# Distance products on half the array's rows each, with operands built by scaled copies

## The reference, cut to what matters

```python
s = x @ w_se.T + b_se                       # 3 numbers a node
sq = jnp.sum(s * s, axis=-1)
dist = sq[:, :, None] + sq[:, None, :] - 2.0 * jnp.einsum('bnd,bmd->bnm', s, s)
A = jnp.exp(-dist) * mask                   # mask: the adjacency, 512 x 512
msg = jax.nn.relu(x @ w_msg.T + b_msg)
x_nmp = jnp.einsum('bnm,bmd->bnd', A, msg)
```

## Time and profile before

| | |
|---|---|
| median of three runs | 655.06 us |
| the profiled execution | 653.34 us |
| its span, first to last instruction | 651.4 us |
| mean granted TensorE clock | 0.986 |
| TensorE matmuls busy | 606.5 us (93%), 3742 instructions |
| TensorE weight loads busy | 522.7 us (80%) |
| VectorE busy | 495.5 us (76%) |
| ScalarE busy | 410.2 us (63%) |
| GpSimd busy | 339.2 us (52%) |

### The profile page before, as it was taken

How to read it: one execution, slowest core, us unless ns; L and a number is a source line. 1 busy time by engine, 2 the same in 40 slices (tenths; PEclk the granted TensorE clock), 3 DMA queues, 4 the chain that set the end, 5 groups by cost and what they waited for, 6 DMA issues and landing times.

```text
span 651.4 us, 12656 instructions
## 1 busy us (share of the span) xinstructions
PE 606.5 (93%) x3742; PEld 522.7 (80%) x3742; DVE 495.5 (76%) x2023; ACT 410.2 (63%) x810; POOL 339.2 (52%) x250
## 2 busy tenths in 40 slices
PE   3899998989899999999999999999999999999990
PEld 2779777877779798989898988788888878999980
DVE  6968888798878888888888898888887856544430
ACT  4654545464849485858585858576676747777760
POOL 3200405042448446666757575748585853555675
PEclk9998999999999999999999999999999999999996
DMA  8427231317283997464665656555656677777553
GB/s 294 150 80 263 77 123 53 98 60 240 61 237 62 280 278 214 92 189 125 151 168 152 166 133 178 141 152 155 169 134 165 175 182 170 174 178 170 115 77 40
DMA packets 91715, 99.63 MB, mean 153 GB/s; under 512 B 7488, under 2 KB 70464, under 8 KB 91328
## 3 DMA queue, kind: packets, MB, share of 16 engines
q1 hardware_dynamic: 69920, 82.30, 40.3%
q0 software_dynamic: 21728, 16.53, 16.7%
HBM read 74.89 MB, written 30.39 MB: 162 GB/s over the span
## 4 chain that ended last, share of the span: by engine, by line
PE 81%; DVE 7%; ACT 5%; issue 4%; POOL 1%; DMA 1%; another core or an unknown queue 1%; POOLq 0%; SPq 0%; DVEq 0%; ACTq 0%
PE G L717 9%; PE Y L607 8%; PE C L541 8%; PE C L539 8%; PE C L540 7%; PE G L539 5%; PE G L541 5%; PE G L540 5%; PE G L607 3%; PE Y L615 3%; PE H L582 2%; PE H L584 2%; PE H L583 2%; PE M L545 2%; PE C L711 2%
## 5 line engine op out<-in xcount | busy, mean ns | idle before, releaser
L988 POOL DMA_INDIRECT out<-y_t,xt x88 | 144.3, 1639 | 117.7 <-DMA out<-y_t,xt 76.7
L1023 POOL DMA_INDIRECT routed<-row,at_u x112 | 126.7, 1131 | 137.1 <-DVE at_u L1220 104.8
L539 PE MATMUL C<-cv_h,w_hi 128*128 128x256 f32 (+1 forms) x432 | 131.7, 305 | 6.2 <-issue 3.7
L540 PE MATMUL C<-cv_l,w_hi 128*128 128x256 f32 (+1 forms) x432 | 125.2, 290 | 0.0
L541 PE MATMUL C<-cv_h,w_lo 128*128 128x256 f32 (+1 forms) x432 | 125.1, 290 | 0.0
L539 PEld LDWEIGHTS C<-cv_h,w_hi 128*128 128x128 f32 x432 | 83.6, 194 | 9.6 <-issue 6.4
L540 PEld LDWEIGHTS C<-cv_l,w_hi 128*128 128x128 f32 x432 | 83.5, 193 | 1.4
L541 PEld LDWEIGHTS C<-cv_h,w_lo 128*128 128x128 f32 x432 | 83.3, 193 | 0.7
L717 PE MATMUL G<-ex,msg_t 128*128 128x512 f32 x128 | 58.9, 603 | 0.3 <-ACT gh L911 0.3
L607 PE MATMUL Y<-ge,w_t 128*128 128x256 f32 x212 | 55.0, 382 | 3.1 <-issue 2.6
L607 PEld LDWEIGHTS Y<-ge,w_t 128*128 128x128 f32 x212 | 37.8, 189 | 12.8 <-issue 9.1
(11 more groups left out here) (265 smaller groups left out, 1679.6 us busy)
## 6 DMA issues: line engine op xcount, KB each, us to landing
w_t<-w_all SPq DMA_DIRECT2D x63, 392.0 KB
adj<-adj_t SPq DMA_DIRECT2D x16, 1024.0 KB
xt<-routed SPq DMA_DIRECT2D x63, 144.0 KB
wd<-w_all SPq DMA_DIRECT2D x11, 392.0 KB
x_ln<-x SPq DMA_DIRECT2D x16, 256.0 KB
x_res<-x SPq DMA_DIRECT2D x16, 256.0 KB
out<-x SPq DMA_DIRECT2D x15, 256.0 KB
w_all<-w_s SPq DMA_DIRECT2D x1, 3136.0 KB, 11.3
```

Of the source, the lines that this page charges most:

```text
L539: pe.matmul(psum, hi(w), rhs_h, start=start, stop=False)
L540: pe.matmul(psum, hi(w), rhs_l, start=False, stop=False)
L988: nc.gpsimd.indirect_dma_start(out=out, out_offset=bass.IndirectOffsetOnAxis(ap=xt[j][:, t, R_ID:R_ID + 1].bitcast(U32), axis=0), in_=y_t[ ...
L1023: nc.gpsimd.indirect_dma_start(out=routed, out_offset=bass.IndirectOffsetOnAxis(ap=ats_u[d % 2][:, n:n + 1], axis=0), in_=rows[d % 2][:, n ...
```

## The change

The eight groups of three rows stand in 32-row blocks 0 and 32 of the first half, and again in the second half. The first block holds s, the second s squared, in each half. ScalarE evicts G2 in four activations of 32 partitions in place of two of 64. The casts become two activations over all 128 partitions with a scale and a bias column from the constants, which also write the constant rows; the VectorE steps become two sums over all partitions. `dist(j)` uses rows 0 to 63 for even j and rows 64 to 127 for odd j, and the wait for `msg_done` stands before `dist(2)`. The two memsets and their semaphore are gone; ScalarE waits once for the constants.

```diff
-S_ROWS = [0, SPACE, 2 * SPACE, 3 * SPACE, 64, 64 + SPACE, 96, 96 + SPACE]
+S_HALF = [0, SPACE, 2 * SPACE, 3 * SPACE, 32, 32 + SPACE, 32 + 2 * SPACE, 32 + 3 * SPACE]
+S_ROWS = [half + row for half in (0, 64) for row in S_HALF]
...
             def dist(j):
-                pe.matmul(DIST[j][:], u_s[:, j * P:(j + 1) * P], v_s[:], start=True, stop=True).then_inc(pe_dist, 1)
+                rows = slice(64 * (j % 2), 64 * (j % 2) + 64)
+                pe.matmul(DIST[j][:], u_s[rows, j * P:(j + 1) * P], v_s[rows, :], start=True, stop=True).then_inc(
+                    pe_dist, 1)
...
-                if is_graph(g, 0):
-                    pe.wait_ge(rows_set, 1)
...
+                pe.wait_ge(msg_done, g + 1)
                 dist(2)
-                pe.wait_ge(msg_done, g + 1)
                 dist(3)
...
-                nc.scalar.activation(s_f[0:64, :], G2[0:64, :], ACT.Identity, bias=vec[0:64, V_SE:V_SE + 1])
-                nc.scalar.activation(s_f[64:P, :], G2[64:P, :], ACT.Square,
-                                     bias=vec[64:P, V_SE:V_SE + 1]).then_inc(s_f32, 1)
+                for half in (0, 64):
+                    places, squares = slice(half, half + 32), slice(half + 32, half + 64)
+                    nc.scalar.activation(s_f[places, :], G2[places, :], ACT.Identity, bias=vec[places, V_SE:V_SE + 1])
+                    last = nc.scalar.activation(s_f[squares, :], G2[squares, :], ACT.Square,
+                                                bias=vec[squares, V_SE:V_SE + 1])
+                last.then_inc(s_f32, 1)
                 tile_results(-1)
                 act.wait_ge(s_f32, g + 1)
-                nc.scalar.copy(u_s[0:96, :], s_f[0:96, :])
-                nc.scalar.copy(v_s[0:64, :], s_f[0:64, :])
-                nc.scalar.copy(v_s[96:P, :], s_f[96:P, :]).then_inc(uv_hi, 1)
+                nc.scalar.activation(u_s[:], s_f, ACT.Identity, scale=cst[:, C_SU:C_SU + 1], bias=cst[:, C_BU:C_BU + 1])
+                nc.scalar.activation(v_s[:], s_f, ACT.Identity, scale=cst[:, C_SV:C_SV + 1],
+                                     bias=cst[:, C_BV:C_BV + 1]).then_inc(uv_hi, 1)
...
             act.wait_ge(vec_loaded, 16)
+            act.wait_ge(cst_loaded, 16)
...
-            def stack(tile, src, pattern, a=0, b=P):
-                return nc.vector.scalar_tensor_tensor(out=tile[a:b, :], in0=tile[a:b, :].bitcast(F32),
-                                                      scalar=cst[a:b, pattern:pattern + 1], in1=src[a:b, :],
-                                                      op0=ALU.mult, op1=ALU.add)
+            def low_halves(tile, scale):
+                return nc.vector.scalar_tensor_tensor(out=tile[:], in0=s_f, scalar=cst[:, scale:scale + 1],
+                                                      in1=tile[:].bitcast(F32), op0=ALU.mult, op1=ALU.add)
...
-                stack(u_s, s_f, C_DU, 0, 96)
-                stack(v_s, s_f, C_DV, 0, 64)
-                stack(v_s, s_f, C_DV, 96, P).then_inc(uv_split, 1)
+                low_halves(u_s, C_AU)
+                low_halves(v_s, C_AV).then_inc(uv_split, 1)
...
-            nc.vector.memset(u_s[96:P, :].bitcast(F32), -0.5)
-            nc.vector.memset(v_s[64:96, :].bitcast(F32), -0.5).then_inc(rows_set, 1)
```

More of the change, by code:

```diff
@@ L85 @@
 C_TRI = C_ID + P
-C_DU = C_TRI + P
-C_DV = C_DU + 1
-C_IOTA = C_DV + 1
+C_SU, C_BU, C_AU, C_SV, C_BV, C_AV = range(C_TRI + P, C_TRI + P + 6)
+C_IOTA = C_AV + 1
 C_HALF = C_IOTA + EXPERTS + 1
@@ L129, in constants @@
     c[:, C_TRI:C_TRI + P] = np.triu(np.ones((P, P)), 1)
[L130 to L134, removed]
+    for row, u, v in zip(S_HALF, ("h", "h", "l", "l", "sh", "sl", "one", "one"),
+                         ("h", "l", "h", "l", "one", "one", "sh", "sl")):
+        for half in (0, 64):
+            at = slice(half + row, half + row + SPACE)
+            for columns, kind in (((C_SU, C_BU, C_AU), u), ((C_SV, C_BV, C_AV), v)):
+                c[at, columns] = {"h": (1.0, 0.0, 0.0), "l": (-1.0, 0.0, 1.0), "sh": (-0.5, 0.0, 0.0),
+                                  "sl": (0.5, 0.0, -0.5), "one": (0.0, 1.0, 0.0)}[kind]
     c[:, C_IOTA:C_IOTA + EXPERTS] = np.arange(EXPERTS)
@@ L305, in gnn_moe @@
         conv_summed = sem("conv_summed")
-        zeroed, rows_set = sem("zeroed"), sem("rows_set")
+        zeroed = sem("zeroed")
         dv_step, dv_pow = sem("dv_step"), sem("dv_pow")
```

## The result

The changed kernel is slower. Its median is 662.84 us (four runs, 659.29 to 666.94), that of the kernel before 655.20 (four runs, 652.9 to 655.95): a ratio of 1.012 with the interval 1.007 to 1.017, or +7.6 us. The forecast was 671.5 (660 to 679): +16.4 on the median of before, where +7.6 was measured. The profiled executions are 659.62 and 653.34 us, +6.3, with spans of 657.8 and 651.4 and a granted clock of 0.986 in both.

The account below looks back on a forecast made before the run. TensorE was taken as the bound, with no slack behind ScalarE's evictions in graphs 6 to 15. 13.7 + 4.3 - 0.7 - 1.8 + 1.7 = +17.2 us on 653.34 gave 670.5, set at 671.5 us (660 to 679).

Parts of the forecast that it names:

- The step that held: Graphs 6 to 15, ScalarE's G2 evictions ahead of L821 and L615: 1.37 us more each, nothing covered, +13.7 us.
- the rival that went faster: G2 evictions cost by partitions, so the stage keeps its length: 644 to 650 us, chance 0.06.
- Its turning point: Added G2 eviction stage at which the faster rival turns: about 0.4 us a graph.
- The products: Four distance products a graph: -0.11 us as middle of -0.46 and +0.24, -1.8 us in 16 graphs.
- The rival that pairing pays in full: Distance products gain all of 7.4 us: 659 to 664 us, still slower, chance 0.20.
- The rival of costly changes of mode: Distance products at +3.8 in place of -1.8, up to one more clock fall: 675 to 679 us, chance 0.12.
- The copies: ScalarE's two scaled copies for three casts: 0.75 us each, 1.50 against 1.79, a gain of 0.29.
- The step that failed: Graphs 2 to 5, TensorE's waits for messages or gelu: each grows by 1.08 us, +4.3 us.
- the clock: Early graphs, TensorE at 1.2 GHz after pauses: one further clock fall, +1.7 us (0 to 5).
- the step's low end: Early graphs' waits: 0 added if the remote event that ScalarE next waits for comes at its own time.
- the sum's base: Profiled execution of the kernel before, 653.34 us, to which the summed +17.2 us was added, giving 670.5.
- Graph 0: VectorE's two sums for three: TensorE's wait for the last falls away in graph 0 only, -0.7 us.

Follow-up runs that it names:

- four_evictions: Kernel before with only its two 64-partition evictions of G2 cut into four of 32 partitions: 664.76 us beside 646.58, ratio 1.028.
- results_mid: Changed kernel with the tile's yT eviction moved between the second and third of the four evictions of G2: 652.42 us beside 646.58, ratio 1.010.
- full_rows: Changed kernel with each distance product over all 128 rows, exponential scale 1: 660.34 us beside 644.40 for the kernel before, ratio 1.025.
- base_third: Kernel before, unchanged, third profile, on a third chip: 653.78 us beside 654.06, ratio 1.000.
- base_again: Kernel before, unchanged, run again for a second profile: 648.78 us beside 646.58, ratio 1.003.
- after_third: Changed kernel, unchanged, third profile, on the same chip as the kernel before's third profile: 663.56 us, ratio 1.014 to the kernel before.
- after_again: Changed kernel, unchanged, run again for a second profile: 662.40 us, ratio 1.025 to the kernel before, +15.8 us.
- four_evictions_b: Kernel before with four 32-partition evictions of G2 in place of two of 64, run again on another chip: 666.87 us, ratio 1.026.

## Why the prediction was right in sign and too large

**The step that held.** L821 and L615 had no slack in graphs 6 to 15, and each added microsecond of ScalarE's stage there became one of TensorE: +1.37 a stage, waits of 1.50, graphs +1.30. four_evictions shows it with that part alone (34.73 - 33.36 = 1.37), results_mid by taking the wait away. The rows were enough to forecast it. Narrower activations cost what wide ones do, 671 and 681 ns for 32 partitions, so the rival that went faster falls. (Its turning point was summed wrongly: by its own terms it lies at (1.8 + 1.2 + 0.7) / 14 = 0.26 us a graph, not at 0.4.)

**The products held.** -0.11 a graph was forecast, -0.08 measured (full_rows). Both bounds' reasons were at work: pairing (-0.45) and the change to half the rows (+0.37). That their sum lies so near the middle is luck, for the middle was taken only because no row told more. The rival that pairing pays in full falls, although its 659 to 664 us held the time: right by its number, for another reason. The rival of costly changes of mode falls too.

**The copies** took 0.80 in place of 0.75, so that stage shrank not by 0.29: from the first copy to the gelu in the changed kernel it is 197.82 - 196.41 = 1.41 against 1.79, -0.38. The second copy starts 0.71 after the first, although each row is 0.80 long. Starts, not durations, add up.

**The step that failed** is the one on the early graphs: +4.3, of which I wrote "I take the full value, for the gap follows directly on ScalarE's last instruction, as if begun by it", with +1.7 for the clock on top. The waits did grow, by 1.13 each. But the gap was not begun by ScalarE's last instruction. It ended with an event at its own time, as the step's low end had it ("if that event comes at its own time, it swallows the delay"). The event can be named. L890 waits for the semaphore, a counter between engines, that TensorE raises with the last product of `conv_sum` (L541); what it needs of VectorE had ended long before (134.87 for the L890 at 139.21). The packed trace holds the time of each raise. The table has it in us from the graph's first eviction of G2, beside the end of what ScalarE does before L890. L541 itself ends at 3.69 in graphs 2 to 4 and at 4.58 in graph 5, in every row (ends on TensorE are modelled).

| | ScalarE free, graphs 2 to 4 | semaphore, graphs 2, 3, 4 | ScalarE free, graph 5 | semaphore, graph 5 |
|---|---|---|---|---|
| before | 4.35 | 5.15, 5.88, 5.87 | 6.64 | 7.95 |
| base_third | 4.35 | 5.15, 5.11, 5.88 | 6.64 | 7.92 |
| base_again | 4.35 | 4.25, 4.29, 4.27 | 6.65 | 7.84 |
| after | 5.49 | 5.13, 5.10, 5.10 | 7.78 | 7.96 |
| after_third | 5.48 | 5.14, 5.12, 5.12 | 7.78 | 7.96 |
| after_again | 5.49 | 4.35, 4.30, 4.26 | 7.78 | 7.87 |
| four_evictions_b | 5.73 | 4.25, 4.27, 4.28 | 8.02 | 7.84 |

The semaphore comes 0.6 to 3.4 us behind the product, and how late goes by the comparison more than by the kernel: after and after_third have it as late as before and base_third mostly do, and do not pause, for their ScalarE gets there after it. In graphs 3 and 4 of before and 4 of base_third it came another 0.75 later, at 5.87 or 5.88; as an estimate, such a one would leave the changed kernel a pause of 5.88 - 5.49 = 0.4. In the four profiles of the second chip it comes 0.01 behind the product, and there graph 5 has no pause in any kernel.

In numbers, for graphs 2 to 5. Without pauses in graphs 2 to 4 and without falls of the clock (after_again against base_again) the change costs +1.8 where +4.3 less 0.4 for the products was forecast: the semaphore swallows graph 5's part, and waits that stood behind the delay another 0.8 in graph 4. The 3.8 us of pauses that before has are no longer there. The clock gave +1.2 where +1.7 was forecast: graphs 2 and 5 of after hold a stretch at the lower level (from 79.7 and 165.0) and take 28.69 and 35.98 where those of after_again take 27.18 and 34.77, together +2.7, against the 1.5 of graph 3 before (111.1). 1.8 - 3.8 + 1.2 = -0.8, as measured. (Outside these graphs, graph 1 has such a stretch only before, from 49.6, which gives 0.6 back; over the early graphs both profiles have two.) Against the sum's +6.0 less 0.4 that is 6.4 of the 10.8 us by which the sum (+17.2) missed the profiled difference (+6.4); the later graphs are another 3.3, graphs 0 and 1 the rest.

**The same in the later graphs.** Nine graphs at +1.30 are +11.7, and graph 15 is another +1.3; measured were +9.3 and 0.0. The kernel before has pauses in graphs 12, 13 and 15 that this profile of the one after lacks, in the timeline of TensorE:

```profile
412.06 1.10 PE L607 MATMUL Y<-ge,w_t 128*128 128x256 f32 x4 [1.19 <-issue]
446.13 1.10 PE L607 MATMUL Y<-ge,w_t 128*128 128x256 f32 x4 [0.52 <-DVE y_t L1320]
513.76 1.10 PE L607 MATMUL Y<-ge,w_t 128*128 128x256 f32 x4 [0.60 <-issue]
```

In the tail a wait for the transfer of xt shrinks besides, from 1.00 to 0.67. The changed kernel is not free of such pauses in other executions: its graphs 10, 11 and 14 take 35.88, 35.16 and 35.75 us in after_again, graphs 8 to 10 35.25, 35.99 and 35.50 in after_third, and in each of the six the same semaphore is 0.8 to 1.2 us behind its product, where in graphs 6 to 15 of the first profile it is at most 0.1 behind. Graphs 6 to 14 are 3.0 and 2.9 us longer there.

I took the execution of before as the sum's base without asking which of its idle times belong to the kernel and which to the execution. Where it has few of them the change costs 15.8 us (after_again), where it has many, 7.6 and 9.5. That the 15.8 stands near the 16.4 that I forecast on the median is luck: the profiled spans of that comparison differ by 12.8, made up of -2.9 in graph 0, where base_again has a fall of the clock (from 27.6) and waits 2.56 us for VectorE, +1.8 in graphs 2 to 5, +13.2 in graphs 6 to 14 and +0.8 in the tail.

**Graph 0** gained 1.34, not 0.7, for a reason that I had not seen. Before, VectorE and GpSimd at 21.5:

```profile
21.42 2.69 POOL L979 TENSOR_TENSOR w_lo<-gates_raw,w_hi 128x1152 fp32r<-128x1152 f32 x1 [3.95 <-ACT w_hi L799]
21.51 2.62 DVE L1531 COPY t_d<-cst 1x8 f32<-1x8 f32 x1
```

and after:

```profile
21.70 0.75 DVE L1094 SCALAR_TENSOR_TENSOR u_s<-ex,cst,u_s 128x512 fp32r<-128x512 f32 x1
22.37 0.74 DVE L1094 SCALAR_TENSOR_TENSOR v_s<-ex,cst,v_s 128x512 fp32r<-128x512 f32 x1
22.40 3.22 POOL L989 TENSOR_TENSOR w_lo<-gates_raw,w_hi 128x1152 fp32r<-128x1152 f32 x1 [5.08 <-ACT w_hi L805]
23.03 2.62 DVE L1124 TENSOR_SCALAR rs<-ve 128x4 int32<-128x4 int32 x1
```

A copy of eight numbers takes 2.62 us while GpSimd does its large sum, and before, the operands' sums stood behind it. ScalarE's later cast starts GpSimd later, and the 2.62 us fall on an operation behind the sums. In the four profiles of the kernel before they fall on one of two small copies, `tid` or `t_d`, both ahead of the sums.

**What stays open.** Why TensorE's semaphore comes up to 3.4 us behind its product, and why that varies with the chip and the execution: no engine and no transfer was found that goes with it. The pauses of the kernel before in graphs 12, 13 and 15 were not followed to such a semaphore. For graphs 2 to 4 no run has four_evictions where the semaphore is 1.4 us or more late; there the argument rests on the two profiles of the changed kernel. Nor is the spread of the changed kernel's own runs explained (657.5 to 668.2 us in three comparisons), for all three of its profiles are of executions under 663 us.

## What to carry to other kernels

Read who is early at the place of the edit: where the consumer starts 0.06 us after the producer's end, and the producer was not waiting for anything either, an added activation counts in full in every iteration, and moving the urgent eviction ahead of the added work gives most of it back. Before a delay is added to a pause that the trace calls remote or issue, see in a second execution whether the pause is there at all, and look up when the semaphore that ends it is raised: if that time does not move with the delayed engine, the pause swallows the delay. Without that, price it from nothing to full. A delayed engine also finds less to wait for behind the delay, so graphs with several small waits pay less than the one wait that grew.

## What the hardware showed that I had not expected

- An activation of 32 partitions by 512 columns takes 671 to 681 ns, one of 64 partitions 683: what is cut in two is paid for twice.
- Two products on separate halves of the rows do run together (0.34 us from pair to pair, 0.27 a product on one half alone), but a group of four among full-row products keeps only 0.08 us of it.
- A VectorE copy of 1x8 takes 2.62 us beside a GpSimd sum of 128x1152 (before, base_again), 0.15 otherwise.
- TensorE's semaphore for the last product of `conv_sum` came 0.6 to 3.4 us behind the product's modelled end in nearly all of graphs 2 to 5 on three chips and in the first comparison, and 0.01 behind it on a fourth chip. A ScalarE that got there later did not wait for it.
- In the same three comparisons one kernel differs by 8.6 us (646.6 to 655.2) and the other by 1.2 (662.4 to 663.6), so the ratio of the two is 1.012 to 1.025.
